# Early-fusion transformer block: start-up of the kernel reordered, and a new hand-out of all engines' instructions

## What is computed

```python
h = tok(x, ln1_g, ln1_b, W, b, ln2_g, ln2_b)      # LN over 768, einsum with W[768,256] + b, LN over 256
h = concatenate([h, txt], axis=1)                 # (64, 196 + 77, 256)
h = h + attn(layernorm(h), Wq..Wo, bq..bo)        # see below
h = h + ffn(layernorm(h), W_r, W_k, W_v, mu_r, mu_k)
# attn: the einsum "nqhd,nkhd->nhqk" of this case mixes, for one token, its 16 heads (16 x 16 scores)
# ffn:  x_prev = x shifted by one token of the image; r = sigmoid(xr W_r), k = relu(xk W_k)^2, out = r * (k W_v)
```

## Time and profile before

| | |
|---|---|
| median of 3 runs | 1607.35 us (1607.32 to 1609.72) |
| profiled execution: time / span | 1607.39 us / 1605.3 us |
| mean granted TensorE clock | 0.951 of full speed |
| busy share TensorE / weight loads / VectorE / ScalarE / GpSimd | 87 / 82 / 77 / 70 / 57% |
| DMA engines' mean busy share | 78.3% on the kernel's queue, 240 MB |

### The profile page before, as it was taken

How to read it: one execution, slowest core, us unless ns; L and a number is a source line. 1 busy time by engine, 2 the same in 40 slices (tenths; PEclk the granted TensorE clock), 3 DMA queues, 4 the chain that set the end, 5 groups by cost and what they waited for, 6 DMA issues and landing times. The chain is left out here.

```text
span 1605.3 us, 51258 instructions
## 1 busy us (share of the span) xinstructions
PE 1399.5 (87%) x17678; PEld 1312.6 (82%) x17678; DVE 1237.2 (77%) x3109; ACT 1120.5 (70%) x2410; POOL 920.5 (57%) x1593
## 2 busy tenths in 40 slices
PE   1568979898999899999899989998999999998976
PEld 1567878788889888988888888898888888888875
DVE  4468777778888788878787888798788888886652
ACT  2357576767876778778767776777677768766754
POOL 2133146557566574765566656655657656666676
PEclk8678989999999999999999999999999999999987
DMA  8149898688898889968986889699897879779830
GB/s 244 40 117 172 167 180 140 141 148 153 173 174 162 134 161 174 167 139 165 176 156 136 178 155 167 132 175 156 170 177 140 172 157 170 151 145 144 163 63 30
DMA packets 687537, 243.43 MB, mean 152 GB/s; under 512 B 589682, under 2 KB 658354, under 8 KB 687154
## 3 DMA queue, kind: packets, MB, share of 16 engines
q1 hardware_dynamic: 687281, 240.16, 78.3%
HBM read 137.18 MB, written 107.94 MB: 153 GB/s over the span
## 5 line engine op out<-in xcount | busy, mean ns | idle before, releaser
L1765 PE MATMUL bank<-wqkv,xnT 128*128 128x384 f32 x1656 | 337.0, 348 | 5.2 <-DVE probs L1492 1.8
L1765 PEld LDWEIGHTS bank<-wqkv,xnT 128*128 128x128 f32 x1656 | 285.1, 191 | 14.2 <-issue 5.5
L1869 PE MATMUL bank<-wtok,xT 128*126 128x258 f32 (+1 forms) x1800 | 255.2, 298 | 0.0
L1869 PEld LDWEIGHTS bank<-wtok,xT 128*126 128x126 f32 (+1 forms) x1800 | 236.9, 200 | 0.0
L1405 POOL TENSOR_TENSOR mixp<-mixf,mixp 128x384 fp32r<-128x384 f32 x184 | 185.2, 1014 | 83.1 <-ACT mixp L1741 82.6
L1662 ACT ACTIVATE arena<-qk,ymask 128x384 f32<-128x384 f32 x368 | 203.2, 609 | 41.5 <-DMA qk<-qkv_dram 31.5
L1683 ACT ACTIVATE xcols<-xim 84x640 f32<-84x640 f32 (+1 forms) x192 | 121.4, 692 | 80.6 <-DVE xs L1511 44.8
L1584 DVE TENSOR_TENSOR qkvt<-bank,bqkv 128x384 f32<-128x384 f32 x276 | 148.7, 546 | 29.8 <-PE bank L1765 20.2
L1420 POOL TENSOR_TENSOR h<-h,r 128x256 f32<-128x256 f32 x138 | 102.0, 743 | 94.7 <-DVE r L1621 93.7
L1349 POOL TENSOR_TENSOR rs<-ve,small 126x1 f32<-126x1 f32 (+1 forms) x192 | 135.1, 704 | 15.0
L1347 POOL TENSOR_TENSOR ve<-mv,small 126x1 f32<-126x1 f32 (+1 forms) x192 | 37.4, 195 | 174.7 <-DVE mv L1545 87.0
(11 more groups left out here) (119 smaller groups left out, 3229.6 us busy)
## 6 DMA issues: line engine op xcount, KB each, us to landing
qkv_dram<-qkvt SPq DMA_DIRECT2D x138, 384.0 KB, 3.4
xim<-in_x SPq DMA_DIRECT2D x128, 294.0 KB
qk<-qkv_dram SPq DMA_DIRECT2D x46, 768.0 KB, 8.3
arena<-qkv_dram SPq DMA_DIRECT2D x368, 48.0 KB
hc<-h_dram SPq DMA_DIRECT2D x45, 384.0 KB, 4.8
out<-h SPq DMA_DIRECT2D x45, 384.0 KB, 3.5
o_dram<-probs SPq DMA_DIRECT2D x108, 96.0 KB, 2.3
on<-o_dram SPq DMA_DIRECT2D x73, 128.0 KB
```

The lines of the kernel that those rows point to most:

```text
L1765: ins = mm(psum, left(a, k), right(b, k), start=t == 0, stop=t == len(terms) - 1)
L1869: ins = mm(place("tok", 0, t)[0:pr, 0:E + 2], xT[:, a, ch, :, :].rearrange("p i w -> p (i w)")[:, r0:r0 + pr], wtok[:, b, ch, :], start=n ...
```

## The change

Six edits:

1. Both `txt` and `load` steps move: `load` of image 0 is step 2, before any text; the four text copies stand at steps 33, 1005, 2285 and 4158 instead of 3, 4, 5 and 7.
2. The start of the DMA queue: `c0b` and the two `ln1_b` vectors get semaphores of their own, so VectorE's scaling waits for the `ln1_g` vectors and the token weights alone. `load_rest(m)` issues `c0b`, `g2b`, `b2b` and three square weights behind image 0 and all the rest behind image 1.
3. The sum of the six parts on VectorE goes; TensorE makes the sum with six products of ones with `scaled`, one as each part is ready. The bias products (`token_bias`) stand behind the second transpose job of image 0.
4. All seven square weights are transposed together at one step, behind `h` of tile 2.
5. In a token tile's group the 18 matmuls come first, and the wait for `x_stats` and the small products of `imask` and `xs` last.
6. For the last chunk, the third tile (no rows) is skipped in `qkv` and `qb` (two jobs), `wo`, `h2`, `r`, `rt`, `val` and `rv`.

Beside these, every row of `AT` and `BANK` is new. Two things can be read from the new table. In the even stretch the token tiles run further ahead: before the last `val` of chunk 20 is issued, 65 token tiles have been, instead of 62; tile 99 is at step 7584 instead of 7761. At the beginning, `tok` of tile 0 stands at step 19 before any step of image 1 (before: step 29, behind two transpose jobs of image 1), and `hin` of chunk 0 at step 87, right behind `hdma` of tile 2 and before `xcols` of image 3 (before: step 94, behind `xcols` of image 3 and `load` of image 4).

```diff
-            return [n for n, v in enumerate(WEIGHTS_AT) if v == s]
+        weights_at = min(AT["h"][0][2] + 1, AT["xt"][0][0])
+            return range(len(WEIGHTS)) if s == weights_at else []
...
-                    sp.dma_start(lnt[:, 6 + 3 * c:9 + 3 * c], ln1_b[...]).then_inc(raw_tok, 16)
-                sp.dma_start(c0b[:, :], tok_b...).then_inc(raw_tok, 16)
+                    sp.dma_start(lnt[:, 6 + 3 * c:9 + 3 * c], ln1_b[...]).then_inc(raw_bias, 16)
...
+            def load_rest(m):
+                if m == 0:
+                    load_vector(c0b[:, :], tok_b, raw_c0)
+                    load_vector(g2b[:, :], ln2_g, raw_ln)
+                    load_vector(b2b[:, :], ln2_b, raw_ln)
+                    for n in range(3):
+                        load_square(n)
+                if m == 1:
+                    for x, v in enumerate((bq, bk, bv)):
+                        load_vector(bnat[:, x, :], v, raw_in)
+                    for n in range(3, 5):
+                        load_square(n)
+                    for n in range(5, 7):
+                        load_square(n)
...
-            dve.wait_ge(prep_dve, c)
-            prep(V.tensor_reduce(wsum, scaled.rearrange("p c e -> p e c"), AX.X, ALU.add))
+            dve.wait_ge(raw_bias, 2 * 16)
...
-            pe.wait_ge(prep_dve, DVE_SUM)
-            mm(banks[SPARE[0]][:, 0:E], ones, wsum, start=True, stop=True).then_inc(prep_pe, 1)
+            for ch in range(KCH):
+                pe.wait_ge(prep_dve, ch + 1)
+                ins = mm(banks[SPARE[0]][:, 0:E], ones, scaled[:, ch, :], start=ch == 0, stop=ch == KCH - 1)
+            ins.then_inc(prep_pe, 1)
...
+                        if job == 1 and m == 0:
+                            token_bias()
...
                 for t in due(s, "tok", 0):
-                    x_stats.wait(pe, m, 1)
+                    x_lo.wait(pe, m, 3 * X_PARTS[m])
                     turn("tok", 0, t)
-                    for m in patch_images(t):
-                        ...imask... xs
-                    x_lo.wait(pe, m, 3 * X_PARTS[m])
...
+                    x_stats.wait(pe, m, 1)
+                    for m in patch_images(t):
+                        ...imask... xs
                     tok_pe.done(ins)
...
+                        if i >= USED[k]:
+                            qkv_pe.skip(pe, k, job)
+                            continue
```

More of the change, by code:

```diff
@@ L767 @@
+        [int(b) for b in "1133477265416022064017164062041374446272545353"],
     ],
     qkv=[
[L769 to L775 removed]
@@ new lines @@
+        [int(b) for b in "4000750610751347166060374622116475751733524430"],
+        [int(b) for b in "2367127202561047413260611632773135027231506621"],
+        [int(b) for b in "5223502617725261656346277374112261325250465405"],
+        [int(b) for b in "6044474303253025360602700117246050546452023256"],
+        [int(b) for b in "4600300317542127432227050145731114502665654310"],
+    ],
+    s=[
+        [int(b) for b in "3362454240644342057173330356374214505761615523"],
+        [int(b) for b in "2421503023315432713707003360662372206375542364"],
+    ],
@@ L787 @@
+    pt=[
+        [int(b) for b in "0202266455556254534665437055177604160014407606"],
+        [int(b) for b in "3532421150311577350133140310176250175020711530"],
+    ],
+    av=[
+        [int(b) for b in "0027331473560710664247144047672425215010161721"],
+        [int(b) for b in "6430413761334752715240327077716130056322727377"],
     ],
     ont=[
-        [int(b) for b in "5152512275251736727233727143532042335313122306"],
-        [int(b) for b in "2636256456023042051074332354704321153224014730"],
-    ],
@@ L805 @@
-    r=[
-        [int(b) for b in "2277006072200375015726766166706446503201660601"],
-        [int(b) for b in "3621347106142266136053007311647377106656403053"],
-        [int(b) for b in "0643256512435024207572235420476026764133227317"],
+        [int(b) for b in "4575000765621720067554370645065351266367466333"],
+        [int(b) for b in "1762116223765364745116716274313435072176200441"],
+    ],
+    wo=[
+        [int(b) for b in "5371423537606241627544070133571301361405024156"],
+        [int(b) for b in "2520000725741620265357225675067565120340515525"],
+        [int(b) for b in "4754265246030374446135336244320052276667672203"],
+    ],
@@ new lines @@
+    zt=[
+        [int(b) for b in "1610403337007213340662010255441026226571615025"],
+        [int(b) for b in "6141561475730746754457205743732343070027472103"],
+    ],
+    k=[
+        [int(b) for b in "0712737731606530521176041262201070603716246642"],
+        [int(b) for b in "3646102227070367443752272315540354256234750771"],
+    ],
+    r=[
+        [int(b) for b in "6662740615431322334066211347563304255530413320"],
+        [int(b) for b in "0255273124671122344075114452013500713256234114"],
+        [int(b) for b in "7407152111666042253017742740234656114133306607"],
@@ L809 @@
     ],
     val=[
-        [int(b) for b in "7336347332102276012720402773450201062025342732"],
-        [int(b) for b in "0454762531336420255355615536367166234707354274"],
-        [int(b) for b in "6720527703117370737403200061544040653726035426"],
+        [int(b) for b in "4531630236060236673154364375602145316304467446"],
+        [int(b) for b in "3064567327604264746767141604112707750617415775"],
+        [int(b) for b in "5637414727440611673321474337324232624530572563"],
     ],
@@ L902 @@
 OUT_ROWS = [min(CT, TOKENS - CT * c) for c in range(CHUNKS)]
+USED = [-(-rows // TT) for rows in OUT_ROWS]
 OUT_DMAS = [1 if rows == CT else -(-rows // TT) for rows in OUT_ROWS]
@@ L932, in done, with skip @@
         return ins
+    def skip(self, eng, k, steps):
+        self.wait(eng, k, steps)
+        eng.sem_inc(self.sem, self.unit)
 class Own:
@@ new lines, in load_rest @@
+            def load_rest(m):
[12 more added lines that the diff above has]
+                        load_square(n)
+                    with nc.allow_non_contiguous_dma(reason="small vectors, once"):
+                        for side, v in ((0, mu_k), (1, mu_r)):
+                            sp.dma_start(mus[:, side, :], v.rearrange("(k p) -> p k", p=128)).then_inc(raw_in, 16)
+                    load_vector(bob[:, :], bo, raw_in)
@@ L1578, in _ @@
                         i, half = job // 2, job % 2
+                        if i >= USED[k]:
+                            qkv_sb.skip(dve, k, job)
+                            continue
                         qkv_pe.wait(dve, k, job + 1)
@@ L1592, in _ @@
                     for k in due(s, "h2", i):
+                        if i >= USED[k]:
+                            h2_sb.skip(dve, k, i)
+                            continue
                         c = k % SLOTS
@@ L1618, in _ @@
                     for k in due(s, "rv", i):
+                        if i >= USED[k]:
+                            rv_sb.skip(dve, k, i)
+                            continue
                         val_pe.wait(dve, k, i + 1)
@@ L1752, in _ @@
                     for k in due(s, "rt", i):
+                        if i >= USED[k]:
+                            r_tanh.skip(act, k, i)
+                            continue
                         r_pe.wait(act, k, i + 1)
@@ L1897, in _ @@
                     for k in due(s, "wo", i):
+                        if i >= USED[k]:
+                            wo_pe.skip(pe, k, i)
+                            continue
                         on_lo.wait(pe, k, 2)
@@ L1917, in _ @@
                     for k in due(s, "r", i):
+                        if i >= USED[k]:
+                            r_pe.skip(pe, k, i)
+                            continue
                         mix_lo.wait(pe, k, 4)
@@ L1922, in _ @@
                     for k in due(s, "val", i):
+                        if i >= USED[k]:
+                            val_pe.skip(pe, k, i)
+                            continue
                         ka_lo.wait(pe, k, 2)
```

82 lines of the change are left out of this document (29 added, 53 removed), and 1098 rows, old and new, of tables (add, av, carry, d).

## The result

The changed kernel takes 1540.9 us (median of 4 runs, 1534.4 to 1550.3), against 1607.3 before: a ratio of 0.960 (95% interval 0.954 to 0.965), 66 us less. The forecast was 33 us less, 1574 (1558 to 1592): the sign is right, the time lies outside the range. The profiled run took 1540.33 us with a span of 1538.4, so 1.9 us lie around it (2.1 before). An execution that ran at a lower granted clock than the others of its kernel is left out of its time; of `a2_middle` this is the profiled one (clock 0.74), so no stretch is read from its trace.

What follows compares the result with a forecast made beforehand. The prediction took TensorE as the bound, 92.3% busy in the middle. From 1607.4 us: -33 (start), -3 (sums last), +4 (texts), 0 (new order), -1 (end) gave 1574, range 1558 to 1592.

Steps and rivals of the forecast that it cites:

- Parts 1 to 3: Start, from image 0 and token weights through images 1 and 2 to first qkv: it comes at 69, 33 us earlier.
- part 1: Start, image 0 and token weights: VectorE's preparation ends at 17.2 instead of 22.30 us, tile 0 starts at 19.5.
- The shift is carried to the end: Behind the first qkv: the start's 33 us arrive whole at the end if the even stretch keeps its density.
- Part 4 (a): Even stretch, patch sums last in the token group: TensorE's 7.6 us wait for them shrinks, gain 3 us (0 to 7.6).
- Part 4 (b): Even stretch, three texts now copied there hold the DMA engines and delay small transfers: cost 4 us (0 to 15).
- Part 4 (c): Even stretch, all else is new order: TensorE's 88 us of idle time stay near 88; 0, bounds -15 and +15.
- 1.5 points: Middle window: the forecast is wrong if TensorE's share, forecast as 92% busy, is off by over this much.
- Part 5: End: nothing lost by earlier token work (bound +4); skipping the last chunk's empty tile gains 1 us (0 to 3).
- C: Rival, middle: longer distances before scores and av also make it denser by 15 of 88 idle us; 1559, chance 0.15.
- B: Rival, middle: texts and shorter distance before wo and k give back part of the gain; 1590, chance 0.17.
- D: Rival, middle: each of some 40 chunks meets one new wait, at wo, 1 us each; 1614, chance 0.05.
- E: Rival, start: images wait for weights, or weights hold back image 3; half the shift stays away; 1590 + a few, chance 0.05.

Runs made afterwards that it cites:

- a2_middle: Start of the kernel before, all four texts at the beginning; from the first qkv on the changed kernel's order, with sums last and skip: 1569.7 us (0.974).
- a1_start: Changed kernel's start but with patch sums first; from the first qkv on the old order, no skip: 1588.2 us (0.987 against the kernel before).
- a5_start_last: Changed kernel's start with patch sums last; from the first qkv on the old order, no skip: 1580.6 us (0.984 against the kernel before).
- b3_text_first: Changed kernel with three text copies ahead of image 0 and the fourth right behind it: 1545.2 us (0.964 against the kernel before).
- a3_text_early: Changed kernel with text copies 1 to 3 moved from the middle to directly behind text 0 in the start: 1537.1 us (0.955 against the kernel before).
- a4_sums_first: Changed kernel with the wait for patch sums and the small products first again in the token group, table unchanged: 1628.5 us (1.012 against the kernel before).
- b1_sums_last: Kernel before with one edit: the 18 matmuls first, wait for patch sums and small products last: 1602.6 us (0.997).
- f2_stat_late: Kernel before with statc, statr and rstd1 moved later, 4.1, 4.3 and 4.7 us of TensorE work behind their tile: 1646.7 us (1.026).
- b2_no_skip: Changed kernel with the third tile of the last chunk worked again: 1541.5 us (0.958 against the kernel before).
- d1: Kernel before with av, rec and osb moved later by up to 5 us of TensorE work: 1657.8 us (1.034).
- d3: As d1, with qk_in and v_in also issued earlier, 15.0 us of TensorE work ahead of the scores instead of 13.2: 1719.8 us (1.069 to 1.077).
- f3: Kernel before with the token tile's whole chain, from sqm to hdma, moved later behind the tile's matmuls: 1718.9 us (1.068).
- c1: Changed kernel with av, rec and osb pulled to directly behind the pt copies, 0.3 and 0.6 us instead of 6.5 and 4.2: 1682.9 us (1.046 against before).
- c3: Changed kernel with av, rec and osb earlier by up to 2.9 us of TensorE work: 1577.7 us (0.984 against the kernel before).
- e1: Changed kernel with the transposes xt and their copies xnh and xnl up to 2.9 us of TensorE work earlier: 1568.8 us (0.977 against the kernel before).
- c2: Changed kernel with qk_in issued later, 12.7 us of TensorE work ahead of the scores instead of 15.6: 1565.0 us (0.972 against the kernel before).
- f1: Changed kernel with sqm, statc and statr earlier, 2.5, 3.3 and 4.2 us behind their tile instead of 4.1, 5.6 and 7.0: 1602.2 us (0.997 against before).
- f4: Changed kernel with sqm alone moved earlier, 2.5 us of TensorE work behind its tile instead of 4.1: 1582.4 us (0.986 against the kernel before).

## Why the prediction was right in the start and wrong in the stretch

**Parts 1 to 3, the shift of the first `qkv`: right.** Timeline of after, columns as the earlier trace rows:

```profile
6.16 1.74 DVE L1455 TENSOR_SCALAR h<-arena,lnt 128x256 f32<-128x256 f32 x6 [6.16 <-POOL wmask L1354]
...
7.82 4.44 DVE L1458 TENSOR_SCALAR qk<-qk,lnt 128x128 f32<-128x128 f32 x6
...
10.12 1.89 ACT L1712 ACTIVATE xcols<-xim 84x640 f32<-84x640 f32 x3 [6.08 <-DMA xim<-in_x]
...
17.90 1.10 DVE L1537 TENSOR_TENSOR xT<-bank,xT 128x420 fp32r<-128x420 f32 x2 [0.17 <-DVE wtok L1472]
...
20.22 3.73 PE L1900 MATMUL bank<-wtok,xT 128*126 128x258 f32 x18 [1.09 <-DVE xT L1537]
21.34 2.02 DVE L1531 TENSOR_REDUCE xs<-xcols 84x14 f32<-84x1792 f32 x1 [1.18 <-ACT xcols L1724]
...
41.31 2.02 DVE L1531 TENSOR_REDUCE xs<-xcols 84x14 f32<-84x1792 f32 x1
45.81 0.38 SPq L1244 DMA_DIRECT2D hc<-h_dram  x1
67.16 1.32 PE L1797 MATMUL bank<-wqkv,xnT 128*128 128x384 f32 x6 [1.32 <-DVE xnT L1595]
```

Image 0's `xcols` were forecast for 9 and began at 10.1; VectorE's preparation ended at 17.9 (17.2); tile 0 began at 20.2 (19.5); sums of image 0 were done at 23.4 (22.7), of image 2 at 43.3 (43.7); `hin` was issued at 45.8 (48); the first `qkv` ran at 67.2 (69). Each step is within 2.2 us. From `hin` to the first `qkv` it took 21.4 us (21); what of this the seven square weights cost was not measured apart. TensorE is idle for 23.6 us before the first `qkv` (forecast about 27; before 60.5).

In part 1 some luck helped. VectorE's six scalings were taken at their old 4.20 us and took 1.74; its six `c0rep` jobs were taken at 1.26 and took 4.44. The two misses, -2.5 and +3.2 us, nearly cancel. And TensorE's sum of the parts did not end 0.7 us behind the last scaling but 3.0 us behind it (10.9 against 7.9); only the slow `c0rep` covered it. The last section shows where the slow jobs come from.

**"The shift is carried to the end": right in the main, with a loss in one run.** By the traces `a1_start` kept all of 22 us (stretch 1503.3) and `a5_start_last` lost 8 of 34. Image 0 ahead of the texts, with which the start was argued, moves the first `qkv` by 10.6 us and the end by 8 to 13 (`b3_text_first` against `a3_text_early`). The sums last move it by 11 to 12 (`a5_start_last`, `a4_sums_first`); the prediction counts them in the start only for tile 0, which it lets begin ahead of its sums (19.5 instead of 22.7). What is left of the start's gain is the other parts together, which no run took apart.

**Part 4 (a), the sums last: the term that was mis-sized, in both directions.** It stands at 3 us. Alone it was worth 0 there (`b1_sums_last`, stretch 1502.8 against 1503.0), as a condition of the new table 75 (`a4_sums_first`, stretch 1546.2 against 1471.2). The prediction saw that the sums stand closer before the group in the new table, and made the gain smaller for it; it was the sign that the table counts on this edit. The two can't be priced one by one and added.

**Part 4 (b), the texts in the middle: 4 us, measured 4 (1541 against 1537)**, with intervals that overlap, so no more than that it is small.

**Part 4 (c), "all else is new order ... I take 0, bounds -15 and +15": the step that failed.** The stretch of the change measured -32, and as the runs give 0, 4 and 0 us for the sums, the texts and the skip in it, (c) itself is about -36; `a2_middle` gives 36 too when the 5 of the sums in the old start are taken off its 41. The 88 us of idle time in the middle are 67 in after (1137.0 - 1069.9), and TensorE's share is 94.1% instead of the forecast 92, more than the 1.5 points that the prediction itself set as a sign of being wrong. Two things were wrong. The bounds of 15 came from no row; the one bound that the rows gave was the idle time itself, 145 us of the stretch. And only TensorE's waits were read. VectorE's 73.9 us for `sel` were in the trace of before, and the distance of `sqm` in the table, 1.2 against 4.1 us, could have been counted like that of `av`; neither gives a size (see `f2_stat_late`), but both say that this order differs where the in-order engines stand.

**Part 5, the end: right that nothing is lost, wrong on the skip's 1 us.** TensorE in the last 101.4 us, before and after:

```profile
1503.90:1605.30 101.40, 73.74 (x798) 68.47 (x796) 45.74 (x108) 54.18 (x118) 67.00 (x90) 0.83 0.33 67
```

```profile
1437.00:1538.40 101.40, 68.61 (x744) 62.62 (x744) 44.22 (x101) 53.06 (x115) 67.13 (x92) 0.80 0.38 67
```

The skip takes 5.1 us of work away, as part 5 has it, and all of it became idle time (27.7 to 32.8 us); `b2_no_skip` agrees. The end waits for the chain of jobs, not for TensorE's work.

**The rivals.** C (the middle gets denser) was the right one, with a chance of 0.15 and half the size (15 of the 32 us); its reason, the distances before scores and `av`, is not shown: losing them costs, adding them to the old order costs too. B, D and E did not come; the longest of TensorE's waits for `o_in` is 2.4 us, in all 13.9 as in the earlier trace rows.

**What stays open.** Which property of the new table makes the stretch 32 us shorter. Steps and banks came together: 1410 of the 1626 banks differ between the two kernels, and no run has the new banks in the old order or the other way round, so a share of the banks in the gain is not excluded. That the gain is in the order from the first `qkv` on is shown (`a2_middle`); that four tries to give the old order one or two properties of the new one, with all else left in place, lose time is shown too (`d1`, `d3`, `f2`, `f3`). Runs that also changed banks (`c1`, `c3`, `d1`, `d3`, `e1`, `f3`) may owe a part of their cost to that; `c2`, `f1`, `f2` and `f4` changed none. A new plan of the old sequence with all properties at once was not tried. No experiment beats the changed kernel by more than the intervals.

## What to carry to other kernels

Split the time at an event that both kernels have (here the first `qkv`), and price the start by following that event and the stretch behind it by its own density: the two halves were 25 and 41 us, and each was measured in a kernel of its own. Where a change brings a planned order together with edits of code, the edits and the order are one term: its gain can be any part of the idle time that there is, not a few us around 0, and an edit that is worth 0 to 5 us alone can be what keeps the order alive (88 us). In an order as full as this one, a kind of job 2 to 3 us of work off its place cost some 20 to 40 us, in `f4_sqm_early` at another place than the wait it made; so read the waits of all in-order engines, and don't expect to better one by moving one kind of job by hand. When two runs are compared, check that they differ in one thing: `b3_text_first` against the change seems to make image 0's place worth 4 us, against `a3_text_early` it is 8 to 13.

## What was not expected of the hardware

VectorE's six scalings of 128 x 256 took 1.74 us, and before 4.20; its six `c0rep` jobs of 128 x 128 took 4.44 us, and before 1.26. Size and form of both are the same in both kernels; only their place in time moved. The traces show what the slow ones have in common: GpSimd's MEMSET of `arena`, 3.3 us long, runs beside them. Timelines of VectorE and GpSimd from 8.1 to 10 us, columns as the earlier trace rows, before, after and in `b2_no_skip`:

```profile
7.70 3.29 POOL L1340 MEMSET arena<- 128x3840 f32 x1
8.40 2.75 DVE L1435 TENSOR_SCALAR h<-arena,lnt 128x256 f32<-128x256 f32 x1 [8.40 <-DMA c0b<-in_L_tok_b]
```

```profile
7.82 3.51 DVE L1458 TENSOR_SCALAR qk<-qk,lnt 128x128 f32<-128x128 f32 x2
7.87 3.32 POOL L1360 MEMSET arena<- 128x3840 f32 x1
```

```profile
7.82 3.36 POOL L977 MEMSET arena<- 128x3840 f32 x1
7.84 3.49 DVE L1072 TENSOR_SCALAR h<-arena,lnt 128x256 f32<-128x256 f32 x1
```

In all three, the VectorE jobs that are under way then, one or two of the six, end 0.15 us behind it (11.15 against 10.99, 11.33 against 11.19, 11.33 against 11.18); the other jobs of the six take 0.2 to 0.3 us each (before, the five behind it take 1.53 us together). In `b2_no_skip` it is the scalings that meet it, 4.97 us in all, and there the first `qkv` comes at 70.6 instead of 67.2 us. No run moved the MEMSET, so what a start without it would gain was not tried.

In `a4_sums_first` TensorE's waiting shows twice: as 53 us more of idle time and as 32 us by which the same work took longer, at a mean granted clock of 0.941 instead of 0.962 of full speed. The ratio of the two clocks, applied to the 1390.7 us of busy time, would give 31 us (an estimate). In `f4_sqm_early`, with idle time up by 34 us (147.7 to 181.9) but at other places, the clock stayed at 0.961 and the busy time rose by 7 us.
